# Two spans of tokens routed from their bare rows in a transformer layer on one core

## The reference, cut to what matters

```python
x = x + attention(layernorm(x))
u = layernorm(x)                                   # (x - mean) / sqrt(var + 1e-5)
probs = softmax(u @ Wr)                            # 8 logits for each token
w_topk, e_topk = top_k(probs, 2)
pos = place of the row in its expert; keep = pos < 512
h = rms(buf, norm_w)                               # an expert's rows, their own norm
buf_out = (gelu(h @ Wg) * (h @ Wu)) @ Wd + buf
combined = u + sum of w_topk * buf_out over the kept choices
fh = rms(u, f_norm)
fout = (gelu(fh @ fWg) * (fh @ fWu)) @ fWd + u
x = x + where(a choice did not fit, fout, combined)
```

## Time and profile before

| what | value |
|---|---|
| median of three runs | 452.97 us |
| the profiled execution's own time | 454.7 us |
| its span, first to last instruction | 453.0 us |
| mean granted clock of TensorE, as a share of 2.4 GHz | 0.945 |
| busy: TensorE, VectorE, ScalarE, GpSimd | 377.0, 309.3, 223.6, 268.0 us |
| chain of waits by engine: TensorE, VectorE, issue, DMA, ScalarE, GpSimd | 53%, 21%, 7%, 7%, 5%, 3% |

### The profile page before, as it was taken

The page is one execution under the profiler, slowest core; times in us unless marked ns, Lnnn a source line. Parts: engine busy times, 40 slices in busy tenths (PEclk is TensorE's granted clock), DMA queues, the critical chain, the costliest instruction groups (busy, mean ns, idle before and its releaser), DMA issues.

```text
span 453.0 us, 7191 instructions
## 1 busy us (share of the span) xinstructions
PE 377.0 (83%) x2419; PEld 178.0 (39%) x2470; DVE 309.3 (68%) x722; ACT 223.6 (49%) x498; POOL 268.0 (59%) x242
## 2 busy tenths in 40 slices
PE   8984879999999999999899889997774496998910
PEld 2432434444334434444335334432334244555510
DVE  3786787857876867777975998874366657655614
ACT  1550343867766667667586755667731121232200
POOL 7374083678559788478587559688603360365550
PEclk9998998999999999999999999999985788999985
DMA  9595675005505009906006000007400012223118
GB/s 226 108 277 134 120 134 103 9 0 105 146 1 106 4 0 208 278 2 109 2 0 108 3 0 9 13 13 222 125 0 20 30 34 72 73 64 84 41 51 275
DMA packets 30461, 37.48 MB, mean 83 GB/s; under 512 B 4757, under 2 KB 25045, under 8 KB 30101
## 3 DMA queue, kind: packets, MB, share of 16 engines
q1 hardware_dynamic: 24378, 29.91, 28.0%
q0 software_dynamic: 2240, 4.21, 3.1%
q10 hardware_dynamic: 3808, 2.92, 2.3%
HBM read 28.56 MB, written 12.75 MB: 91 GB/s over the span
## 4 chain that ended last, share of the span: by engine, by line
PE 53%; DVE 21%; issue 7%; DMA 7%; ACT 5%; POOL 3%; SPq 2%; DVEq 0%; ACTq 0%; POOLq 0%
PE ps_av L1132 13%; PE ps_st L1103 11%; PE ps_slot L1024 10%; DVE neg_max L1353 6%; PE ps_slot L1028 4%; ACT probs L914 3%; PE ps_st L1209 2%; PE ps_slot L1163 2%; DMA k_parts<-part_all 2%; DMA x_sb<-in_L_attn_x_dram 2%; PE ps_av L1211 2%; PE ps_st L1111 1%; POOL probs L734 1%; PE ps_slot L1066 1%; DVE probs L1660 1%
## 5 line engine op out<-in xcount | busy, mean ns | idle before, releaser
L914 ACT ACTIVATE probs<-ps_st 128x512 f32<-128x512 f32 (+3 forms) x384 | 168.4, 494 | 104.0 <-PE ps_st L1103 97.2
L1353 DVE TENSOR_REDUCE neg_max<-ps_slot 128x1 f32<-128x640 f32 (+7 forms) x184 | 175.8, 989 | 56.2 <-PE ps_slot L1028 54.3
L734 POOL TENSOR_TENSOR probs<-probs,f_all 128x960 f32<-128x960 f32 (+2 forms) x65 | 123.8, 1904 | 10.3 <-ACT probs L914 5.4
L1024 PE MATMUL ps_slot<-k_stack,q_stack 128*128 128x512 bf16 (+3 forms) x366 | 96.0, 329 | 11.4 <-DVE neg_max L1353 6.2
L1103 PE MATMUL ps_st<-q_stack,k_stack 128*128 128x512 bf16 (+3 forms) x369 | 99.5, 327 | 5.6 <-ACT probs L914 4.1
L1132 PE MATMUL ps_av<-probs,v_all 128*9 128x512 f32 (+3 forms) x768 | 81.2, 497 | 2.7 <-POOL probs L734 1.6
L731 POOL TENSOR_SCALAR_AFFINE_SELECT probs<-probs 128x512 f32<-128x512 f32 x58 | 37.2, 641 | 68.7 <-ACT probs L914 68.5
L1028 PE MATMUL ps_slot<-b_all,flip_b 128*128 128x240 bf16 (+2 forms) x288 | 66.3, 255 | 1.0 <-DVE neg_max L1353 0.5
L1103 PEld LDWEIGHTS ps_st<-q_stack,k_stack 128*128 128x128 bf16 x384 | 34.5, 97 | 76.2 <-ACT probs L914 54.5
L1024 PEld LDWEIGHTS ps_slot<-k_stack,q_stack 128*128 128x128 bf16 x384 | 36.0, 99 | 44.0 <-DVE neg_max L1353 12.3
L739 POOL DMA_INDIRECT slots<-token_rows,slot_no x32 | 32.5, 1015 | 34.1 <-DVEq L1541 26.1
(11 more groups left out here) (188 smaller groups left out, 405.9 us busy)
## 6 DMA issues: line engine op xcount, KB each, us to landing
q_stack<-q_parts SPq DMA_DIRECT2D x21, 192.0 KB
slots<-in_c_rows_dram SPq DMA_DIRECT2D x4, 528.0 KB, 10.0
probs<-slots SPq DMA_DIRECT2D x8, 264.0 KB
parts<-in_c_rows_dram SPq DMA_DIRECT2D x4, 512.0 KB, 9.8
q_stack<-parts SPq DMA_DIRECT2D x4, 512.0 KB, 5.5
k_stack<-k_parts SPq DMA_DIRECT2D x14, 128.0 KB
f_all<-g_vec ACTq DMA_DIRECT2D x1, 1536.0 KB, 11.4
q_parts<-part_all SPq DMA_DIRECT2D x16, 96.0 KB, 3.3
```

What stands on the lines that cost most here:

```text
L734: pool.tensor_tensor(pr, pr, f_of[:, n % (H // HG), :, fo:fo + hi - lo], ALU.mult).then_inc(near_done, 1)
L914: act.activation(probs[:, u % PBUF, g, c0:512], ps_st[:, ST_NO[what] % 3, c0:512], ACT.Exp, scale=SCALE).then_inc(exp_done, 1)
L1024: pe.matmul(ps_slot[:, slot, o + lo:o + hi], q_stack[:, buf, t // MT, g, t % MT * P:(t % MT + 1) * P], k_stack[:, buf, lo // CW, g, 0:hi - ...
L1353: dve.tensor_reduce(neg_max[:, t // MT, heads[0]:heads[-1] + 1, t % MT], src, AX.X, ALU.max, negate=True).then_inc(slot_used, 1)
```

## The change

Six things change.

1. A new item "RC" behind unit 60 takes the mean of each column from the router: TensorE multiplies it with a matrix of 1/128 (`ones_f`, which GpSimd fills at the start), and VectorE subtracts (`router_c`).
2. For spans two and three the logits come from the bare rows: "XC" turns the rows of `x_sb` as they stand behind the addition of "B", ScalarE copies them, and "D" multiplies with `router_c`; VectorE scales with the layer norm's inverse root. The normed rows are still made, but by ScalarE ("U", with a bias that the new item "UB" makes on VectorE), and turned ("C") only for the fallback. "RI" moves behind "POS".
3. For span two the items from "A" to the choice of experts stand in step eight, ahead of the last units' factor products; before, its "C", "D" and the choice stood partly in step eight and partly behind it. The "Y" of step eight's first half comes earlier in its unit.
4. The scaling of the fallback's weights ("FW") and of the weights of experts 0 and 1 ("FOLD") stands behind the last "Y".
5. "WARM" has 4 and 4 matmuls in place of 10 and 6.
6. The second pass over `x1` waits for each quarter of the fallback's products, in place of all.

A dispatch also waits for the normed rows of its span.

```diff
-    (92, 1, ("A", 2)), (92, 3, ("B", 2), ("BN", 2, 0), ("BN", 2, 1)),
-    (94, 0, ("RS", 1, 0), ("RS", 1, 1), ("RS", 1, 2), ("RS", 1, 3)), (94, 3, ("NEAR", 10)),
-    (95, 0, ("U", 8), ("U", 9), ("U", 10), ("U", 11)), (95, 3, ("NEAR", 11)))
+    (91, 3, ("A", 2)), (92, 1, ("B", 2), ("BN", 2, 0), ("BN", 2, 1)), (92, 2, ("RS", 1, 0), ("RS", 1, 1)),
+    (92, 3, ("XC", 2), ("RS", 1, 2), ("RS", 1, 3), ("UB", 1)), (93, 2, ("D", 1)), (94, 0, ("MX", 1, 0), ("IX", 1, 0)),
+    (94, 1, ("CHOOSE", 1, 0), ("CHOOSE", 1, 1)), (94, 2, ("CHOOSE", 1, 2), ("CHOOSE", 1, 3), ("X", 1)),
+    (94, 3, ("NEAR", 10), ("CHOOSE", 1, 4)), (95, 3, ("NEAR", 11)))
...
-    + [("C", 2), ("AV", NG - 1, NU - 3), ("RI", 1), ("D", 1), ("AV", NG - 1, NU - 2)] + choose(1) \
-    + [("AV", NG - 1, NU - 1), ("EVAC", NG - 1, 1), ("Y", NG - 1, 1), ("PR", 1)] + place(1) \
-    + [("A", 3), ("B", 3), ("WARM", 10), ("BN", 3, 0), ("BN", 3, 1)] + [("RS", 2, j) for j in range(4)] \
-    + [("U", t) for t in range(TT - CH, TT)] + [("RI", 2), ("C", 3), ("D", 2), ("WARM", 6)] + choose(2) + [("PR", 2)] + place(2)
+    + [("U", t) for t in range(TPB, TPB + CH)] + [("AV", NG - 1, NU - 3), ("PR", 1), ("AV", NG - 1, NU - 2)] + place(1) \
+    + [("RI", 1), ("AV", NG - 1, NU - 1), ("EVAC", NG - 1, 1), ("Y", NG - 1, 1)] \
+    + [("FOLD", 0), ("FOLD", 1), ("FW",), ("A", 3), ("B", 3), ("WARM", 4), ("XC", 3), ("BN", 3, 0), ("BN", 3, 1)] \
+    + [("RS", 2, j) for j in range(4)] + [("UB", 2), ("D", 2), ("C", 2), ("WARM", 4)] + [("U", t) for t in range(TT - CH, TT)] \
+    + choose(2) + [("C", 3), ("PR", 2)] + place(2) + [("RI", 2)]
...
             if u == Y_AT[0]:
-                rows[HG - 1].append(("Y", n, 0))
+                rows[HG - 1 if n < NG - 1 else 1].append(("Y", n, 0))
...
                 if t in SPAN_STARTS and k == 0:
                     pool.wait_ge(rows_ready, SPAN_STARTS[t] + 1)
+                    pool.wait_ge(u_done, SPANS[SPAN_STARTS[t]][1])
...
                 if t == 0:
                     act.wait_ge(roots_done, 1)
+                elif t >= TPB and t % CH == 0:
+                    act.wait_ge(last_bias, t // CH - 1)
                 act.activation(u_rows[:, t, 0:C], x_sb[:, t, :], ACT.Identity, bias=xn_bias[:, t:t + 1],
                                scale=rstd[:, 1, t:t + 1]).then_inc(u_done, 1)
...
+                elif kind == "XC":
+
+                    act.wait_ge(slot_full, SLOT_NO["B", 2] + 1 if what[1] == 2 else SLOT_NO["D", 1] + 1)
+                    evacuate(what, x1T)
...
+                elif kind == "XC":
+                    pe.wait_ge(slot_used, SLOT_NO["B", c] + 1)
                 else:
                     pe.wait_ge(u_done, CH * (c + 1))
...
+                if kind == "RC":
+                    pe.wait_ge(late_in, 48)
+                    pe.wait_ge(fixed, 2)
+                    mm = pe.matmul(ps_slot[:, slot, 0:E_NUM], ones_f[:, :], router[:, :], start=True, stop=True)
...
+                        rows, weights = uT[:, tile * P:(tile + 1) * P], router
+                        if c >= 1:
+                            rows, weights = x1T[:, t * P:(t + 1) * P], router_c
...
+                if b >= 1:
+                    scale = rstd[:, 0, SPANS[b][0]:SPANS[b][1]].rearrange("p (t a) -> p t a", a=1)
+                else:
+                    scale = arr3(RINV)
...
+            def last_biases(b):
+                r = slice(*SPANS[b])
+                dve.scalar_tensor_tensor(out=xn_bias[:, r], in0=mv[:, r, 0], scalar=-1.0, in1=rstd[:, 1, r],
+                                         op0=ALU.mult, op1=ALU.mult).then_inc(last_bias, 1)
+
+            def scale_fallback():
+                dve.wait_ge(fw_in, 48)
+                dve.wait_ge(late_in, 48)
+                dve.tensor_scalar(fw[:, 0:2 * F4], fw[:, 0:2 * F4], fn_col[:, 0:1], None, ALU.mult).then_inc(fw_done, 1)
+
+            def fold_norm(e, i):
+                if e < 2:
+
+                    dve.wait_ge(ew_in, 48)
+                    dve.wait_ge(av_done, NG * NU)
+                else:
+                    dve.wait_ge(gu_ps, 2 * (e - 1))
...
-            dve.wait_ge(f_ps, NCH)
             for t in range(TT):
+                dve.wait_ge(f_ps, t // CH + 1)
                 dve.wait_ge(base1, t + 1)
...
-            dve.wait_ge(ew_in, 48)
-            fold_norm(0, 0)
-            fold_norm(1, 1)
             weights_of_rows(0, 0, 0)
```

72 lines of the change are left out of this document (40 added, 32 removed).

## The result

The changed kernel takes **450.55 us** (median of 20 runs, 447.81 to 454.66) beside 453.68 us for the kernel before (20 runs): ratio 0.993, 95% interval 0.9907 to 0.9954, so 3.1 us shorter. Forecast were 445.9, with a range from 442.2 to 449.4. The sign was right and the size was less than half of the 7.1 us that I forecast; the time lies outside the range.

A forecast was written before the change was run, and what follows sets the result against it. Attention until 328 us was taken as TensorE-bound, then a chain of short steps with engines waiting on each other. First expert product 7.3 us earlier, less 0.2 for the router's mean: 452.97 - 7.1 = 445.9 us, range 442.2 to 449.4.

The forecast's parts named there:

- Places to first expert product: From span three's places to the first expert product: dispatches become the bound by 1.4 us, 12.0 us until SyncE's load, product at 372.5.
- If SyncE's load leaves later than 368.5: Sign set in advance: the prediction is wrong if the load of the experts' rows leaves after 368.5 (356.4 + 12.0).
- The change doesn't touch: The eight experts, from first product to the end, were to keep their 73.2 us.
- another clock: Sign set in advance: the prediction is wrong if the experts take another time than 73.2 us, for instance at another clock.
- Addition to logits: Span three, from the last addition of "B" to its logits: 9.13 us become 5.15, 4.0 us gained, the largest term.
- The third rival: Dispatches slow TensorE between "A" and the router's product, costing 7.0 us, perhaps the fallback too: 456.6 us, chance 0.03.
- "Y" 1.7 us earlier: End of attention: with span two routed earlier, "Y" ends at 341.5, 1.7 us earlier; bounds no gain and 3.5.
- Logits to places: Span three: normed rows and their turn ahead of the counts' product add 0.5 us to 5.10; bounds 0 and 2.6.
- The weights scaled ahead: Five VectorE instructions hidden in the wait behind "Y"; the turn to first expert product shrinks from 2.69 to 1.41 us.
- The rule weighed: The skill's rule that activity releases TensorE's throttled clock was set aside; the half clock was kept for 336 to 338.
- The second rival: TensorE's clock stays at 2.4 GHz from the last sums to the logits, 3.5 us saved: 442.4 us, chance 0.22.
- The base: The starting time: the profiled span of 453.0 us, equal to the three runs' median 452.97, from which the shift was taken.

The follow-up runs named there:

- y0: The changed kernel run and profiled once more, unaltered: 450.77 us, ratio 0.9941 to the kernel before.
- w2: The changed kernel, unaltered, on the same chip as w1 for comparison: 450.1 us, ratio 0.9934 to the kernel before.
- y3: The changed kernel with span two routed behind the last units as before, still from bare rows: 450.55 us, ratio 0.9943.
- z1: The changed kernel with the whole fallback, and so both passes over x1, held until all dispatches have landed: 459.4 us.
- z2: The changed kernel with only VectorE's two passes over x1 held until all dispatches have landed: 454.5 us.
- z3: x1 with 18 instead of 8 warming matmuls between the fallback and the first turn of experts' rows: 448.86 us, ratio 0.9913.
- x1: The changed kernel with the eight warming matmuls before span three's logits written out instead of two loops: 448.73 us, ratio 0.9905.
- x4: The changed kernel with the last four dispatches of span two held until the logits of span three: 450.32 us, ratio 0.9942.
- x3: The changed kernel with all eight dispatches of span two held until the logits of span three: 453.83 us, ratio 1.0019.
- w1: v4 with 14 instead of 8 warming matmuls ahead of the first turn of experts' rows: 445.31 us, ratio 0.9842.
- y2: The kernel before with only the fallback's and first two experts' weights scaled ahead of the last "A": 453.57 us, ratio 0.9985.
- y1: x1 with span three's rows normed directly behind their bias and turned ahead of the choice: 450.04 us, ratio 0.9952.
- v1: The changed kernel with only the second pass over x1 held until all dispatches have landed: 451.48 us.
- v4: x1 with the first pass over x1 for tiles 0 to 7 moved behind the scaled weights, joined with y1's early normed rows: 449.26 us, ratio 0.9896.
- z4: y3 with span two routed from normed rows, so bare rows for span three alone: 452.89 us, ratio 1.0023.
- x2: The changed kernel with the eight warming matmuls before span three's logits left out: 449.5 us, ratio 0.993.

## Why the prediction missed

Three steps failed. Counted over y0 and w2, the way from addition to logits took 1.8 us longer than forecast, the way from places to load 1.5, and the experts 1.4. That "Y" ended 0.8 us earlier than forecast took part of this back, by luck: the place in step eight, from which I had worked it out, has no part in it that y3 shows.

1. **"Places to first expert product" failed.** I took 12.0 us to SyncE's load from a profile in which the first pass over x1 began beside the third-last dispatch and no dispatch was lengthened:

```profile
369.54 1.40 DVE L1612 SCALAR_TENSOR_TENSOR x_sb<-token_rows,x_sb 128x128 f32<-128x128 f32 x5
...
371.35 0.98 POOL L739 DMA_INDIRECT slots<-token_rows,slot_no  x1 [0.30 <-issue]
```

I made the dispatches the bound in the same step and put their cost beside other work at nothing. In the changed kernel the pass began earlier against them (362.43, beside the last four), and 12.0 became 13.6. z1 and z2 give 11.95 and 11.94 without the passes, so the 12.0 was right for dispatches alone. "If SyncE's load leaves later than 368.5" was the mark that I had set (356.4 + 12.0 is 368.4); it left at 369.85.
2. **"The change doesn't touch" the experts' 73.2 us.** They took 74.4 to 74.7 in three profiles: the first products run at the half clock, 0.54 and 0.50 in six us, where before had 0.75. At the full clock 71.7 or 71.8 (z1, z2, z3). The prediction named another clock as a way to be wrong and gave it no term.
3. **Addition to logits, 5.15 us, "the largest term", failed by the most.** Without the late signal it measured 5.4 at the half clock (x1, x4), 4.6 at the full clock (x3, w1), so the engines' own work was sized rightly. But I took the product as seen when it ends; beside the dispatches VectorE, ready, still waited 2.0 to 3.4 us for it. In the changed kernel the way is 7.0, and 8.4 once. The third rival had this in its kind, dispatches that hold up TensorE, at 7.0 us for that stretch where 2.0 to 3.4 were measured.
4. **"Y" 1.7 us earlier.** It ended 2.4 to 3.9 us earlier than in the one profile of before, and 0.7 to 2.3 earlier than in y2. With span two routed behind the last units it was 122.6 all the same (y3), so most of my working went into a place that bought nothing.
5. **Logits to places, 0.5 more than before.** Unhidden it is 2.5 more (7.6 in x1, 5.1 before), at the upper bound, since ScalarE's exponential and TensorE's counts both stand behind the normed rows, and 1.1 us of late signal stand ahead of those in x1. With the rows moved ahead it was 5.3 (y1). In the changed kernel the late logits hid it, so it cost 0.6 there.
6. **The weights scaled ahead** were hidden, and the turn to the first product took 1.4 (y0, w2) or 1.7 us, as worked out.
7. **The rule weighed.** In the kernel before, the granted clock from 336 to 338 was 0.50 with TensorE busy for 2.00 us; in the first profile after, it was 1.00 with 1.28 us busy:

```profile
336.00:338.00 2.00, 1.28 (x24) 1.00 0.00 0
```

By the rule of the Trainium skill ("TensorE: Matmul & The Clock Gate", section "What's actually happening") that activity releases the throttle, the busier stretch should have had the higher level; neither profile bears that out here, and the level moves from one execution to the next (y0 fell to 0.50 at 339.6, x1 at 343.8). The second rival, a full clock, did come true in the first profile up to the addition, 3.5 us ahead of my forecast as its sum said, and the late logits took 3.4 back.
8. **The base.** The profile of before ran 1.0 us over the median of its 20 runs (454.7 against 453.68). I took its span, which happened to equal the first three runs' median, as the median's equal; the shift counted from the second addition is 3.0, so this moved the base and not the shift. I also read the slices of the earlier trace rows wrongly: TensorE is busy for 7 tenths from 306 us on and not from 328, and the tenths from 328 on are 7, 4, 4, 9, 6. No term of the sum hangs on that.

## What to carry to other kernels

When a change makes another queue the bound, reprice that queue with what will now run beside it: here 12.0 us of dispatches became 13.6 when VectorE's pass over two SBUF operands fell further into them. The same goes for what the queue's work does to others: dispatches beside a chain of short steps held up the signals between them. A gain at one wait is worth what the next wait leaves of it, so follow the order on every engine up to the next meeting point; the normed rows that were put ahead of the counts ate 2 us of what x1 had won. And count from a fixed event shared by both kernels, over several profiles, before a difference of 1 us is believed.

## What the runs showed of the hardware

- **The signal that an instruction has ended can come late beside indirect DMAs.** Six profiles (first, y0, w2, z1, z2, v1) show VectorE ready and waiting 2.0 to 3.4 us for a product of TensorE shown as ended; the wait ended 1.4 to 1.6 us after the last dispatch. v4 and z4 show it with VectorE's own instructions, whose ends are measured (2.05 us once, four waits of 0.38 to 1.26 us). Without dispatches the logits did not wait (x3). In before the logits began 0.7 us behind their product, beside dispatches; what decides it is open.
- **A dispatch of 0.97 us took 1.05 to 2.11** beside VectorE's first pass over x1, and in the last span never without it; not each one beside it did. Where the last dispatch took 1.10, the load sometimes left 2.4 to 2.65 us behind it instead of 1.2 (first, w2, v1; not x2).
- **The granted clock of the same stretch differs between executions of one kernel**: 1.00, 0.50 and 0.50 for the turn of the last "A" in three profiles of the changed kernel (first, y0, w2), worth 1.4 us between "Y" and the last addition (2.8 against 4.2).
